# Causal mask of the row maxima in the 16-wide attentions: by TensorE on every own piece instead of by VectorE

## The chip, the cores and the metric

One core of a Trainium2 chip runs the whole program. The metric is the device time of one execution in microseconds; the table below gives the median of three runs. TensorE does the matrix products and writes PSUM, VectorE and ScalarE work on PSUM and SBUF, GpSimd on SBUF, and SyncE issues the copies.

## What is computed

The reference is a chain of sixteen layers on 1024 tokens (batch folded to one in this kernel) of width 256, each with a layer norm ahead and the input added behind. Four of them contain the same kind of attention, with 16 heads of 16 elements: layer 0a, the feed-forward 0 (which runs twice and has an attention inside), and layer 3a. Cut to what matters:

```python
Q, K, V = split_heads(x @ Wq.T), split_heads(x @ Wk.T), split_heads(x @ Wv.T)
scores = jnp.einsum('bhqd,bhkd->bhqk', Q, K) / jnp.sqrt(jnp.float32(HEAD_DIM))
scores = jnp.where(causal, scores, jnp.float32(-jnp.inf))
attn = jax.nn.softmax(scores, axis=-1)
out = jnp.einsum('bhqk,bhkd->bhqd', attn, V)
```

For the softmax the kernel needs the maximum of each row of the masked scores. That maximum is what the change is about.

## The kernel before, in words

narrow_attention() is called once for each of the four attentions, as L0a, L0f (twice) and L3a. It splits queries and keys into three bf16 parts, stacks the parts with copies into qs and ks, and then works in eight units. A unit is a quad of four heads and a half of 512 queries; QUAD_UNITS gives their order. For each unit there are two kinds of work:

- Row maxima. piece() on TensorE makes the scores of 128 queries against up to 512 keys in a bank of a ring of three to four, in bf16 with 96 rows of contraction. find_max() on VectorE reduces the bank to one maximum for each row and frees it. max_pieces() lists the pieces of a unit: for a second half 16 pieces against all the earlier keys, and for every unit 11 own pieces, against the keys of its own half. Own pieces hold a diagonal block and so need the causal mask. The first query tile has one own piece with four heads of 128 keys, the second has two with two heads of 256 keys, the third and fourth have one for each head, with 384 and 512 keys. So there are 8 own pieces of a single head in each unit. part_max() on VectorE then splits a unit's maxima into three bf16 parts, turn_max() (t0 to t7) transposes them on TensorE, keep_max() copies them out and SyncE writes them under qs (place_max()), so that the later scores already have the maximum taken off.
- Scores, exponentials, values. score() on TensorE makes a tile of 128 keys against the queries in one of three banks (s and x in the order), weigh() on ScalarE takes the exponentials, and add_values() on TensorE multiplies them with the values (a in the order), in f32.

The order of all of it is written by narrow_order() as a list of names, which each engine walks through, taking its own part. The pieces m0, m1, ... of a unit stand among the scores of the unit before it; those of units 0 and 1 stand among the projections (p) and values (v) at the start. Around the third own query tile of unit 4 the order reads, with the masked single-head pieces m95 to m102:

```python
m95 s38 m96 x38 m97 s39 x39 m98 s40 m99 x40 m100 s41 m101 x41 a18 a19 m102 s42 x42
```

In unit 5 the same stretch is m122 to m129 and has the four transposes r2 between m124 and m125; unit 3 has r0 in that place. In unit 6 the masked pieces are m133 to m140, of which one stands to about two scores. In unit 7 the order is `m144 a36 a37 m145 m146 s78 m147 s79 m148 s80 m149 x80 m150 s81 x81 a38 a39 m151 s82`. The start reads `p5 m3 m4 m5 p6 m6 m7 m8 v1 m9 m10 p7 m11 v2 m12 m13 t0 m14 m15 m16 v3 m17 m18 m19 m20 s0 x0`; m3 to m10 are the masked single-head pieces of unit 0, m14 to m21 those of unit 1.

Before the change the mask of an own piece is put on in two ways. Pieces with several heads get it on TensorE: behind each head's matmul comes another, ident_bf times causal, added into the last 128 columns (line 1066). Pieces of a single head get it on VectorE: find_max() (line 1358) adds a slice of the tile late to the scores, writes the sums to late_scores and keeps the running maximum. All other pieces are reduced by a plain maximum (line 1362). load_input() makes the constants on GpSimd in the first stage.

Of the kernel before, what the change touches and what calls it, by code (L numbers as in the profile page):

```python
# [6 lines left out]
ALU = mybir.AluOpType  # L7
ACT = mybir.ActivationFunctionType
AX = mybir.AxisListType.X
# [14 lines left out]
class Core:  # L24


    def __init__(self, nc, dram, whole):
        self.nc = nc
        self.dram = dram
        self.old = []  # L30
        self.count = 0
        self.next = self.entered = None
        self.lead = 0
        self.psum = whole.enter_context(nc.psum_tensor("psum", [P, 8, HALF], F32))

        def sb(name, shape, dt=F32):
            return whole.enter_context(nc.sbuf_tensor(name, shape, dt))

        self.x = sb("x", [P, NT, D])
        self.hT = sb("hT", [P, DC, TOK])  # L40
        self.h = sb("h", [P, NT, D])
        self.stats, self.mv = sb("stats", [P, NT, 6]), sb("mv", [P, NT, 2])
        self.scale, self.shift = sb("scale", [P, NT]), sb("shift", [P, NT])
        self.zeros = sb("zeros", [P, HALF], BF16)
        self.powers = sb("powers", [P, 2 * NT])
        self.ident = sb("ident", [P, P])
        self.ident_bf = sb("ident_bf", [P, P], BF16)
        self.causal = sb("causal", [P, P], BF16)
        self.causal_turned = sb("causal_turned", [P, P], BF16)
        self.ones = sb("ones", [P, P])  # L50
        self.late = sb("late", [P, HALF])
        self.ones_rows = nc.dram_tensor("ones_rows", (3, HEADS * TOK), BF16).ap()


# [294 lines left out]
def load_input(core):  # L349

    nc, x = core.nc, core.x
    with Stage(core, "load") as st:
        loaded = [st.sem(f"loaded{q}") for q in range(4)]
        zeroed, ones_set = st.sem("zeroed"), st.sem("ones_set")
        rows_set, rows_stored, powers_set = st.sem("rows_set"), st.sem("rows_stored"), st.sem("powers_set")
        rows = st.sb("rows", [3 * HEADS, TOK], BF16)
        pairs = [st.pair(), st.pair()]
        bank = [core.bank(pairs[q // 2] + q % 2) for q in range(4)]
        following = core.next.open(st, groups=PAIRS, kept_by_dve=(0, 2), last_by_dve=False)
        block = st.opened  # L360

        @block.sync
        def _(sp):
            for q in range(4):
                two = slice(2 * q, 2 * q + 2)
                sp.dma_start(x[:, two, :], core.dram["x"].rearrange("(t p) d -> p t d", p=P)[:, two, :]
                             ).then_inc(loaded[q], 16)
            following.load(sp)
            sp.wait_ge(rows_set, 1)
            sp.dma_start(core.ones_rows.rearrange("i (h t) -> (i h) t", t=TOK), rows[:]).then_inc(rows_stored, 16)  # L370
            sp.wait_ge(rows_stored, 16)
            following.finish(sp)

        @block.vector
        def _(dve):
            nc.vector.memset(core.powers[:, 0:NT], -0.5).then_inc(powers_set, 1)
            nc.vector.memset(core.powers[:, NT:2 * NT], 0.5).then_inc(powers_set, 1)
            nc.vector.memset(rows[:], 1.0).then_inc(rows_set, 1)
            for q in range(4):
                following.find_spread(dve, q, loaded[q])  # L380
            for q in range(4):
                following.keep_dve(dve, q, bank[q])

        @block.scalar
        def _(act):
            for q in range(4):
                act.wait_ge(loaded[q], 16)
                following.row(act, q)
                if q in (1, 3):
                    following.keep_act(act, q, bank[q])  # L390

        @block.tensor
        def _(pe):
            pe.wait_ge(ones_set, 3)
            for q in range(4):
                following.turn(pe, q, bank[q])

        @block.gpsimd
        def _(pool):
            nc.gpsimd.memset(core.ident[:], 0.0).then_inc(zeroed, 1)  # L400
            nc.gpsimd.memset(core.late[:], 0.0).then_inc(zeroed, 1)
            nc.gpsimd.memset(core.ident_bf[:], 0.0).then_inc(zeroed, 1)
            nc.gpsimd.memset(core.causal[:], 0.0).then_inc(zeroed, 1)
            nc.gpsimd.memset(core.causal_turned[:], 0.0).then_inc(zeroed, 1)
            nc.gpsimd.memset(core.ones[:], 1.0).then_inc(ones_set, 1)
            pool.wait_ge(zeroed, 5)
            nc.gpsimd.affine_select(out=core.late[:, HALF - P:], in_=core.late[:, HALF - P:], compare_op=ALU.is_ge,
                                    fill=MASKED, base=0, pattern=[[-1, P]], channel_multiplier=1
                                    ).then_inc(ones_set, 1)
            for t in (core.ident, core.ident_bf):  # L410
                nc.gpsimd.affine_select(out=t[:], in_=t[:], compare_op=ALU.not_equal, fill=1.0, base=0,
                                        pattern=[[-1, P]], channel_multiplier=1).then_inc(ones_set, 1)

            nc.gpsimd.affine_select(out=core.causal[:], in_=core.causal[:], compare_op=ALU.is_ge, fill=MASKED,
                                    base=0, pattern=[[-1, P]], channel_multiplier=1).then_inc(ones_set, 1)
            nc.gpsimd.affine_select(out=core.causal_turned[:], in_=core.causal_turned[:], compare_op=ALU.is_ge,
                                    fill=MASKED, base=0, pattern=[[1, P]], channel_multiplier=-1
                                    ).then_inc(ones_set, 1)
            nc.gpsimd.memset(core.zeros[:], 0.0).then_inc(ones_set, 1)
            pool.wait_ge(powers_set, 2)  # L420
            for q in range(4):
                following.find_scale(pool, q)
            pool.wait_ge(ones_set, 7)


def early(core, stack, name, loads):
# [403 lines left out]
def narrow_attention(core, name, loaded, bias=False, factor=None, first_gated=None):  # L830
# [14 lines left out]
    with Stage(core, name) as st:  # L845
# [21 lines left out]
        whole = [weights[4][:, n, :] for n in range(2)]  # L867
        pool_rest = weights[5][:, 0, :]
        piece_max = [st.sb(f"piece_max{n}", [P, 2, 4, 4]) for n in range(2)]
        late_scores = [st.sb(f"late_scores{n}", [P, HALF]) for n in range(3)]  # L870
        lowest, left = st.sb("lowest", [P, 16]), st.sb("left", [P, 16])
        max_parts = [st.sb(f"max_parts{n}", [P, 3, 16], BF16) for n in range(2)]
        max_rows = [st.sb(f"max_rows{n}", [3 * 16, P], BF16) for n in range(2)]
# [145 lines left out]
        def _(pe):  # L1019
# [31 lines left out]
            def piece(n):  # L1051
                u, i, kh, j0, heads, width = PIECES[n]
                q, half = QUAD_UNITS[u]
                if n == FIRST_PIECE[u]:
                    pe.wait_ge(stacked[q, half], STACKED)
                    if half:
                        pe.wait_ge(stacked[q, 0], STACKED)
                to = own_bank(f"m{n}")
                masks = kh == half and heads > 1
                for e in range(heads):  # L1060
                    h = 4 * q + j0 + e
                    a, b = e * width, (e + 1) * width
                    last = nc.tensor.matmul(to[:, a:b], qs[0:SPLIT, half, h, i * P:(i + 1) * P],  # L1063
                                            ks[0:SPLIT, kh, h, 0:width], start=True, stop=not masks)
                    if masks:
                        last = nc.tensor.matmul(to[:, b - P:b], core.ident_bf[:], core.causal[:],
                                                start=False, stop=True)
                last.then_inc(ring_full, 1)
# [252 lines left out]
        def _(dve):  # L1321
# [28 lines left out]
            def find_max(n):  # L1350
                u, i, kh, j0, heads, width = PIECES[n]
                posted(dve, f"m{n}")
                own = kh == QUAD_UNITS[u][1]
                to, src = piece_max[u % 2][:, int(own), j0:j0 + heads, i], bank_of(f"m{n}")[:, 0:heads * width]
                if own and heads == 1:
                    if n >= 3:
                        taken(dve, f"m{n - 3}")
                    nc.vector.tensor_tensor_reduce(out=late_scores[n % 3][:, 0:width], in0=src,
                                                   in1=core.late[:, HALF - width:], scale=1.0, scalar=-3.0e38,
                                                   op0=ALU.add, op1=ALU.max, accum_out=to).then_inc(ring_free, 1)  # L1360
                else:
                    nc.vector.tensor_reduce(to, src.rearrange("p (e k) -> p e k", e=heads), AX, ALU.max  # L1362
                                            ).then_inc(ring_free, 1)

            def part_max(u):

# [2886 lines left out]
```

## Time and profile before

| | |
|---|---|
| median of 3 runs | 2865.28 us (2863.52 to 2867.5) |
| the profiled execution, its own time | 2867.31 us |
| its span in the profile | 2865.6 us |
| mean granted clock of TensorE | 0.986 of full speed |
| busy: TensorE, VectorE, ScalarE, GpSimd | 95%, 61%, 47%, 24% |
| masked passes on VectorE (line 1358) | 256, and 256 reads of the accumulator |
| mask matmuls on TensorE for the maxima (line 1066) | 256 |

The span is what the profiler saw between the first and the last instruction. A busy TensorE is not one at its peak: the entry of a matmul lasts from its start to its modelled end, and neighbours overlap, so the distance of two starts tells what one costs when they follow closely. "PEld" is the loading of weights, which overlaps the matmuls.

### The profile page before, as it was taken

What the parts mean: (1) busy time and instruction counts of PE and PEld (TensorE: products, weight loads), DVE (VectorE), ACT (ScalarE), POOL (GpSimd) and SP (SyncE); (2) the same over time, 40 slices, a digit from 0 to 9 for tenths busy, and PEclk for the clock granted to TensorE, in tenths of its full rate; (3) what the DMA queues carried; (4) which work ended last, traced back from release to release, by engine and by line L of the source; (5) the groups of instructions that cost most, each with busy time, mean ns of one, the idle gap of its engine ahead of it and who ended that gap; (6) DMA issues with size and microseconds to landing.
All of it is one profiled execution on the core that took longest, in us unless ns stands there. A gap on an engine that the chain in (4) does not pass through costs nothing. (4 is left out here: it accounts for less than half of the span.)

```text
span 2865.6 us, 45708 instructions
## 1 busy us (share of the span) xinstructions
PE 2711.4 (95%) x16625; PEld 1924.5 (67%) x16625; DVE 1735.6 (61%) x3723; ACT 1358.3 (47%) x2811; POOL 677.0 (24%) x815
## 2 busy tenths in 40 slices
PE   7989998989999998999999999899999999989979
PEld 4444465744576886788788888776767677754545
DVE  7758545677446765766666666653333332487487
ACT  3745633536534433433555555543433342336476
POOL 3012002030001532333211110113333330130185
PEclk9999999999999999999999999999999999999999
DMA  3021010020110530432100000000000000120031
GB/s 98 25 58 63 2 52 29 1 65 28 34 33 28 155 111 24 131 111 71 32 23 16 21 16 18 15 26 12 18 12 17 12 36 14 41 69 24 13 101 56
DMA packets 72697, 122.27 MB, mean 43 GB/s; under 512 B 16158, under 2 KB 47232, under 8 KB 72336
## 3 DMA queue, kind: packets, MB, share of 16 engines
q1 hardware_dynamic: 70876, 118.04, 13.7%
q8 instruction: 135, 2.21, 0.3%
q10 hardware_dynamic: 1600, 1.31, 0.3%
q14 instruction: 86, 0.70, 0.1%
HBM read 92.21 MB, written 1.54 MB: 33 GB/s over the span
## 5 line engine op out<-in xcount | busy, mean ns | idle before, releaser
L130 PE MATMUL psum<-L1f_hT_part,L1f_wide 128*128 128x512 f32 x1104 | 269.2, 393 | 10.3 <-DVE L1f_inner L2792 6.1
L236 POOL TENSOR_TENSOR scale<-scale,powers 128x1 f32<-128x1 f32 (+1 forms) x98 | 57.5, 586 | 855.4 <-DVE scale L217 855.4
L1702 ACT ACTIVATE L2b_tanh<-psum,L2b_inverse 128x512 f32<-128x512 f32 x192 | 110.7, 580 | 269.5 <-PE psum L1650 268.1
L130 PEld LDWEIGHTS psum<-L1f_hT_part,L1f_wide 128*128 128x128 f32 x1104 | 201.5, 188 | 54.8 <-DVE L1f_inner L2792 10.7
L2600 POOL TENSOR_TENSOR L1f_inner<-L1f_inner,L1f_weight 128x512 f32<-128x512 f32 x96 | 144.1, 1508 | 263.9 <-DVE L1f_inner L2792 178.0
L1281 ACT ACTIVATE L0f_weights<-psum 128x512 f32<-128x512 f32 (+2 forms) x320 | 157.0, 565 | 95.4 <-PE psum L1097 75.2
L1659 PEld LDWEIGHTS psum<-L2b_v,L2b_weights 128*128 128x128 f32 x1152 | 141.3, 193 | 40.2 <-issue 28.7
L130 PE MATMUL psum<-L1f_down,L1f_inner_part 128*128 128x256 f32 x1152 | 154.3, 285 | 7.8 <-DVE L1f_down L2803 4.2
L130 PEld LDWEIGHTS psum<-L1f_down,L1f_inner_part 128*128 128x128 f32 x1152 | 150.2, 193 | 15.1 <-DVE L1f_inner_part L2808 9.3
L2731 ACT ACTIVATE L1f_gate<-psum 128x512 f32<-128x512 f32 x96 | 57.4, 598 | 211.4 <-PE psum L130 182.5
L2808 DVE TENSOR_TENSOR L1f_inner_part<-L1f_inner,L1f_inner_part 128x512 fp32r<-128x512 f32 x96 | 147.5, 1546 | 9.7 <-ACT L1f_inner_part L2752 9.4
L1650 PE MATMUL psum<-L2b_q,L2b_k 128*128 128x512 f32 (+3 forms) x384 | 149.9, 487 | 1.0 <-DVE L2b_q L1768 0.8
L1659 PE MATMUL psum<-L2b_v,L2b_weights 128*128 128x129 f32 x1152 | 145.2, 278 | 5.8 <-POOL L2b_weights L1568 5.8
L2279 ACT CAST L2a_probsT<-psum 128x512 fp32r<-128x512 f32 (+3 forms) x128 | 65.0, 508 | 147.4 <-PE psum L2131 147.3
L130 PE MATMUL psum<-L2a_k,L2a_q 128*128 128x512 f32 (+3 forms) x576 | 130.7, 356 | 1.7 <-DVE L2a_k L2352 0.9
L2362 DVE TENSOR_REDUCE L2a_negmax<-psum 128x1 f32<-128x512 f32 (+7 forms) x128 | 95.2, 753 | 57.9 <-PE psum L2118 57.8
L1063 PE MATMUL psum<-L0f_ks,L0f_qs 96*128 96x512 bf16 (+3 forms) x384 | 111.5, 332 | 9.9 <-DVE L0f_piece_max L1362 5.6
L2792 DVE TENSOR_TENSOR L1f_inner<-psum,L1f_gate 128x512 f32<-128x512 f32 x96 | 65.9, 689 | 88.8 <-ACT L1f_gate L2731 82.4
L1633 PE MATMUL psum<-hT,L2b_early 128*128 128x512 f32 x248 | 116.5, 593 | 0.9 <-PEq L103 0.9
L1362 DVE TENSOR_REDUCE L0f_piece_max<-psum 128x1 f32<-128x512 f32 (+2 forms) x176 | 108.9, 682 | 12.1 <-PE psum L1063 7.5
L1094 PE MATMUL psum<-L0f_qs,L0f_ks 99*128 99x512 bf16 (+3 forms) x384 | 112.1, 328 | 3.2 <-ACT L0f_weights L1281 2.1
L130 PE MATMUL psum<-L2a_probsT,L2a_v 128*128 128x512 f32 (+3 forms) x576 | 111.6, 348 | 0.7 <-DVE L2a_probsT L2372 0.7
(573 smaller groups left out, 6478.6 us busy)
## 6 DMA issues: line engine op xcount, KB each, us to landing
L1f_w<-in_L1f_w SPq DMA_DIRECT2D x32, 384.0 KB, 3.6
L1f_weight<-combine SPq DMA_DIRECT2D x32, 384.0 KB, 4.4
L1f_weight<-combine SPq DMA_DIRECT2D x32, 256.0 KB, 4.6
scan_spread_b<-bc SPq DMA_DIRECT2D x16, 512.0 KB, 3.7
L0f_qs<-L0f_part SPq DMA_DIRECT2D x96, 64.0 KB, 2.6
experts_early<-in_L1f_w SPq DMA_DIRECT2D x16, 384.0 KB, 4.4
L2b_early<-in_L2b_w SPq DMA_DIRECT2D x16, 384.0 KB, 3.0
L0f_ks<-L0f_part SPq DMA_DIRECT2D x86, 64.0 KB, 2.6
```

What stands on the lines that cost most here:

```text
L130: last = nc.tensor.matmul(to, stationary, moving, start=start and n == 0, stop=stop and n == len(pairs) - 1, skip_group_check=skip)
L1063: last = nc.tensor.matmul(to[:, a:b], qs[0:SPLIT, half, h, i * P:(i + 1) * P], ks[0:SPLIT, kh, h, 0:width], start=True, stop=not masks)
L1094: last = nc.tensor.matmul(to, ks[:, kt // 4, h, kt % 4 * P:(kt % 4 + 1) * P], qs[:, half, h, at:], start=True, stop=not masks)
L1281: nc.scalar.activation(to, src, ACT.Exp, scale=HD ** -0.5).then_inc(exped, 1)
L1362: nc.vector.tensor_reduce(to, src.rearrange("p (e k) -> p e k", e=heads), AX, ALU.max).then_inc(ring_free, 1)
L1633: last = nc.tensor.matmul(to[:], w[e][:, c, at:at + P], hT[:, c, half * HALF:(half + 1) * HALF], start=(c == 0), stop=(c == DC - 1))
L1650: nc.tensor.matmul(ps_scores[u % 3][:, at:], k[e][:, kt * P:(kt + 1) * P], q[e][:, half * HALF + at:(half + 1) * HALF], start=True, stop=T ...
L1659: last = nc.tensor.matmul(ps_out[t % 2][:, 0:P + 1], weights[UNITS.index((kt, t // 4))][:, at:at + P], v[e][:, kt, :], start=(kt == 0), st ...
L1702: nc.scalar.activation(tanhs[u % 3][:, at:], ps_scores[u % 3][:, at:], ACT.Tanh, scale=inverse[e][:, NT + kt:NT + kt + 1]).then_inc(capped, 1)
L2362: nc.vector.tensor_reduce(negmax[:, i:i + 1], ps_scores[i % 2][:, 0:width(i)], AX, ALU.max, negate=True).then_inc(maxed, 1)
L2600: nc.gpsimd.tensor_tensor(inner[u % INNER][:], inner[u % INNER][:], weight[n % SPREAD][:, half * HALF:(half + 1) * HALF], ALU.mult).then_i ...
L2808: nc.vector.tensor_tensor(low[:], inner[u % INNER][:], high[:], ALU.subtract).then_inc(inner_low, 1)
```

## The change

core.late and late_scores go, with their two instructions in the first stage (a memset and a select on GpSimd). piece() puts the mask matmul behind every own piece, those of a single head too; find_max() reduces every piece by the plain maximum. The order of work stays as it is.

```diff
--- before.py
+++ after.py
@@ -48,7 +48,6 @@
         self.causal = sb("causal", [P, P], BF16)
         self.causal_turned = sb("causal_turned", [P, P], BF16)
         self.ones = sb("ones", [P, P])
-        self.late = sb("late", [P, HALF])
         self.ones_rows = nc.dram_tensor("ones_rows", (3, HEADS * TOK), BF16).ap()
 
 
@@ -391,22 +390,18 @@
 
         @block.tensor
         def _(pe):
-            pe.wait_ge(ones_set, 3)
+            pe.wait_ge(ones_set, 2)
             for q in range(4):
                 following.turn(pe, q, bank[q])
 
         @block.gpsimd
         def _(pool):
             nc.gpsimd.memset(core.ident[:], 0.0).then_inc(zeroed, 1)
-            nc.gpsimd.memset(core.late[:], 0.0).then_inc(zeroed, 1)
             nc.gpsimd.memset(core.ident_bf[:], 0.0).then_inc(zeroed, 1)
             nc.gpsimd.memset(core.causal[:], 0.0).then_inc(zeroed, 1)
             nc.gpsimd.memset(core.causal_turned[:], 0.0).then_inc(zeroed, 1)
             nc.gpsimd.memset(core.ones[:], 1.0).then_inc(ones_set, 1)
-            pool.wait_ge(zeroed, 5)
-            nc.gpsimd.affine_select(out=core.late[:, HALF - P:], in_=core.late[:, HALF - P:], compare_op=ALU.is_ge,
-                                    fill=MASKED, base=0, pattern=[[-1, P]], channel_multiplier=1
-                                    ).then_inc(ones_set, 1)
+            pool.wait_ge(zeroed, 4)
             for t in (core.ident, core.ident_bf):
                 nc.gpsimd.affine_select(out=t[:], in_=t[:], compare_op=ALU.not_equal, fill=1.0, base=0,
                                         pattern=[[-1, P]], channel_multiplier=1).then_inc(ones_set, 1)
@@ -420,7 +415,7 @@
             pool.wait_ge(powers_set, 2)
             for q in range(4):
                 following.find_scale(pool, q)
-            pool.wait_ge(ones_set, 7)
+            pool.wait_ge(ones_set, 6)
 
 
 def early(core, stack, name, loads):
@@ -867,7 +862,6 @@
         whole = [weights[4][:, n, :] for n in range(2)]
         pool_rest = weights[5][:, 0, :]
         piece_max = [st.sb(f"piece_max{n}", [P, 2, 4, 4]) for n in range(2)]
-        late_scores = [st.sb(f"late_scores{n}", [P, HALF]) for n in range(3)]
         lowest, left = st.sb("lowest", [P, 16]), st.sb("left", [P, 16])
         max_parts = [st.sb(f"max_parts{n}", [P, 3, 16], BF16) for n in range(2)]
         max_rows = [st.sb(f"max_rows{n}", [3 * 16, P], BF16) for n in range(2)]
@@ -1056,7 +1050,7 @@
                     if half:
                         pe.wait_ge(stacked[q, 0], STACKED)
                 to = own_bank(f"m{n}")
-                masks = kh == half and heads > 1
+                masks = kh == half
                 for e in range(heads):
                     h = 4 * q + j0 + e
                     a, b = e * width, (e + 1) * width
@@ -1352,15 +1346,8 @@
                 posted(dve, f"m{n}")
                 own = kh == QUAD_UNITS[u][1]
                 to, src = piece_max[u % 2][:, int(own), j0:j0 + heads, i], bank_of(f"m{n}")[:, 0:heads * width]
-                if own and heads == 1:
-                    if n >= 3:
-                        taken(dve, f"m{n - 3}")
-                    nc.vector.tensor_tensor_reduce(out=late_scores[n % 3][:, 0:width], in0=src,
-                                                   in1=core.late[:, HALF - width:], scale=1.0, scalar=-3.0e38,
-                                                   op0=ALU.add, op1=ALU.max, accum_out=to).then_inc(ring_free, 1)
-                else:
-                    nc.vector.tensor_reduce(to, src.rearrange("p (e k) -> p e k", e=heads), AX, ALU.max
-                                            ).then_inc(ring_free, 1)
+                nc.vector.tensor_reduce(to, src.rearrange("p (e k) -> p e k", e=heads), AX, ALU.max
+                                        ).then_inc(ring_free, 1)
 
             def part_max(u):
```

## Rows read from the trace of the kernel before

**Rows 1.** The page, part 1: busy time, share of the span, instructions.
```profile
PE 2711.4 (95%) x16625; PEld 1924.5 (67%) x16625; DVE 1735.6 (61%) x3723; ACT 1358.3 (47%) x2811; POOL 677.0 (24%) x815
```

**Rows 2.** Windows of the first two 16-wide attentions; last columns granted clock, DMA share, GB/s.
```profile
28.00:168.00 140.00, 131.83 (x1000) 63.72 (x999) 107.64 (x284) 86.00 (x177) 11.82 (x12) 1.00 0.16 51
203.00:353.00 150.00, 140.43 (x1007) 65.62 (x1008) 111.54 (x290) 86.49 (x179) 24.14 (x24) 0.97 0.15 40
```

**Rows 3.** Waits in 28:168: who for whom, total us, times, longest.
```profile
DVE L0a_late_scores L1358 <- PE psum L1063: 18.7, 18, 2.2
...
PEld psum L1094 <- ACT L0a_weights L1281: 12.7, 32, 1.3
```

**Rows 4.** Groups by line and form in 28:168: busy, mean ns, idle before.
```profile
L1362 DVE TENSOR_REDUCE L0a_piece_max<-psum 128x1 f32<-128x512 f32 x64 | 39.5, 682 | 2.6 <-PE psum L1063 2.6
...
L1358 DVE CUSTOM_DVE_ANT_0 L0a_late_scores<-psum,late 128x512 f32<-128x512 f32 x32 | 20.8, 688 | 8.0 <-PE psum L1063 7.9
...
L1358 DVE DVE_READ_ACCUMULATOR2_ANT L0a_piece_max<- 128x1 f32 x64 | 5.3, 82 | 0.0
```

**Rows 5.** Timeline, VectorE: start, duration, instruction, idle before.
```profile
93.43 6.67 DVE L1362 TENSOR_REDUCE L0a_piece_max<-psum 128x1 f32<-128x512 f32 x11 [0.53 <-PE psum L1063]
...
106.53 0.69 DVE L1358 CUSTOM_DVE_ANT_0 L0a_late_scores<-psum,late 128x512 f32<-128x512 f32 x1
107.14 0.08 DVE L1358 DVE_READ_ACCUMULATOR2_ANT L0a_piece_max<- 128x1 f32 x1
107.14 0.69 DVE L1358 CUSTOM_DVE_ANT_0 L0a_late_scores<-psum,late 128x512 f32<-128x512 f32 x1
```

**Rows 6.** Timeline, TensorE, a piece with four heads of 128 keys.
```profile
99.52 0.22 PE L1063 MATMUL psum<-L0a_ks,L0a_qs 96*128 96x128 bf16 x1
99.58 0.22 PE L1066 MATMUL psum<-causal,ident_bf 128*128 128x128 bf16 x1
99.63 0.22 PE L1063 MATMUL psum<-L0a_ks,L0a_qs 96*128 96x128 bf16 x1
```

**Rows 7.** Timeline, TensorE and ScalarE, unit 4; then unit 5's first masked piece.
```profile
103.48 0.34 PE L1063 MATMUL psum<-L0a_ks,L0a_qs 96*128 96x384 bf16 x1
103.65 0.38 PE L1094 MATMUL psum<-L0a_qs,L0a_ks 99*128 99x512 bf16 x1
...
104.07 4.03 ACT L1281 ACTIVATE L0a_weights<-psum 128x512 f32<-128x512 f32 x8 [1.61 <-PE psum L1094]
...
104.42 0.69 PE L1094 MATMUL psum<-L0a_qs,L0a_ks 99*128 99x512 bf16 x2
...
104.95 0.33 PE L1063 MATMUL psum<-L0a_ks,L0a_qs 96*128 96x384 bf16 x1
...
109.58 2.26 ACT L1281 ACTIVATE L0a_weights<-psum 128x384 f32<-128x384 f32 x5 [1.48 <-PE psum L1097]
...
124.81 0.34 PE L1063 MATMUL psum<-L0a_ks,L0a_qs 96*128 96x384 bf16 x1
```

**Rows 8.** Timeline, unit 6 (TensorE) and unit 7 (ScalarE).
```profile
137.44 0.39 PE L1094 MATMUL psum<-L0a_qs,L0a_ks 99*128 99x512 bf16 x1 [0.22 <-ACT L0a_weights L1281]
...
155.18 2.97 ACT L1281 ACTIVATE L0a_weights<-psum 128x256 f32<-128x256 f32 x6 [1.87 <-PE psum L1097]
```

**Rows 9.** Timeline, TensorE, pieces of units 0 and 1 among the projections.
```profile
34.17 0.76 PE L1063 MATMUL psum<-L0a_ks,L0a_qs 96*128 96x384 bf16 x3
...
42.45 0.34 PE L1063 MATMUL psum<-L0a_ks,L0a_qs 96*128 96x384 bf16 x1 [0.29 <-DVE L0a_piece_max L1362]
```

**Rows 10.** Timeline, TensorE, the first score of unit 2.
```profile
73.47 0.38 PE L1094 MATMUL psum<-L0a_qs,L0a_ks 99*128 99x512 bf16 x1 [0.86 <-DMA L0a_qs<-L0a_max_rows]
```

**Rows 11.** Timeline, GpSimd, its first work after the constants.
```profile
4.99 0.71 POOL L236 TENSOR_TENSOR scale<-scale,powers 128x2 f32<-128x2 f32 x1 [1.11 <-DVE scale L217]
```

**Rows 12.** Timeline, TensorE, the same values in the first and second attention.
```profile
69.24 1.71 PE L1112 MATMUL psum<-L0a_weights,L0a_v 128*32 128x512 f32 x16
...
252.44 3.21 PE L1112 MATMUL psum<-L0f_weights,L0f_v 128*32 128x512 f32 x16
```

## The prediction

> **What bounds the kernel now.** I read the page first. TensorE is busy for 95% of the span, VectorE for 61%, ScalarE for 47% [rows 1]. That is a mean over sixteen layers; the change touches only the four 16-wide attentions, so the next view is their windows, some 150 us each; two of the four are shown [rows 2]. In the first, TensorE is busy 131.8 of 140 us, VectorE 107.6 and ScalarE 86.0. No engine is full, so the chain passes between them, and the timeline has to say who waits at each masked piece.
>
> A masked piece is one head's 128 queries against 384 or 512 keys: PIECES holds eight for each of eight units, so 64 in an attention and 256 in the kernel. Across all of them in the first attention VectorE stood idle 18.7 us in 18 waits for their matmul [rows 3]. At these pieces VectorE mostly waits for TensorE. That is the first sign that moving work from VectorE to TensorE is moving it the wrong way.
>
> **What VectorE is relieved of.** Now a masked maximum is two entries: the pass (688 ns for 512 columns) and a read of the accumulator (82 ns); a plain maximum of 512 is one entry of 682 ns [rows 4]. By duration the change saves 0.688 + 0.082 - 0.682 = 0.09 us a piece, 256 x 0.09 = 23 us of busy time. But durations overlap. Back to back, masked passes of 512 start at 106.53 and 107.14, 0.61 apart; the accumulator read at 107.14 starts together with the next pass [rows 5]. Eleven plain maxima in a row take 6.67 us: (6.67 - 0.68)/10 = 0.60 apart [rows 5]. So where VectorE works without a pause a piece is cheaper by about 0.01 us, and where it works alone the end moves from start + 0.61 + 0.08 = 0.69 to start + 0.68, again 0.01. No row shows a plain maximum of 384, half of the cases; as the fixed part is the same, I take the same 0.01 for it. Bounds: 0.01 and 0.09 us a piece. I take 0.01, since the starts show it directly.
>
> **What TensorE gets.** Each masked piece gains a 128-column matmul of ident_bf and causal with its weight load. The same pair stands already behind the narrow pieces: at 99.52 a piece of 128, at 99.58 its mask, at 99.63 the next piece [rows 6]. That is 0.057 us a step; the entry's 0.22 is latency, and the weight load lies under the matmul before it. No row shows a mask behind a piece of 384 or 512; the bounds are this 0.057 and twice as much, 0.114, the price at half the clock (rows 12 show the clock's effect); I take the step, the nearest row. Total: 64 x 0.057 = 3.65 us an attention, 256 x 0.057 = 14.6 us. The Trainium skill, "TensorE: Matmul & The Clock Gate", section "Back-to-back issue gap", puts a sustained stream of load and matmul pairs of 128 columns at about 81 ns each; by that the total would be 20.7 us. The rows disagree with 0.057, and the measurement decides.
>
> **How much of the 3.65 us is on the path**, unit by unit in the first attention.
>
> *Unit 4* (pieces m95 to m102), step by step [rows 7]. m95 at 103.48 stands ahead of the first score at 103.65, and ScalarE's burst of eight exponentials starts at 104.07 after 1.61 us of idling for that score: 0.057 passes through. The next two pieces come ahead of the second score of the row at 104.42; it starts at 104.42 + 0.69 - 0.38 = 104.73, held by ScalarE, where the array was free at 104.42 + 0.22 = 104.64. With this 0.09 of slack the shift there is 3 x 0.057 - 0.09 = 0.08. m98 (104.95) is again followed by a score held by ScalarE: back to ScalarE's own 0.057. From then on a 384-column step of 0.17 (103.48 to 103.65) makes 0.22 for 512 columns, and a period is piece 0.22, score 0.22, mask 0.057 = 0.50, against ScalarE's (4.03 - 0.6)/7 = 0.49: no slack. m99, m100 and m101 each add 0.057, making 0.23 as TensorE reaches the values. The values need exponentials long finished, so they start 0.23 late; m102 follows, and the score behind it ends ScalarE's idle 1.48 us at 109.58: 0.285 late. Less 0.01 for VectorE: 0.28 of 0.46 us.
>
> *Units 3 and 5* are alike but have four transposes (r0 in unit 3, r2 between m124 and m125 in unit 5), which take away ScalarE's lead; four pieces in place of three then add in full: 0.36 each. *Unit 7*: m145 and m146 stand ahead of the score that ScalarE has idled 1.87 us for at 155.18 [rows 8], and from there to the values the order holds one piece to each score, so that every mask adds: 0.45. *Unit 6* has few pieces for each score; TensorE waits for ScalarE behind them (0.22 at 137.44, rows 8), and only those just behind the values count: 0.20. *Unit 0* lies between projections, with VectorE waiting for its pieces; its three pieces at 34.17 take 0.76 us, where two steps of 0.16 and an end of 0.33 would be 0.65, so some 0.13 is slack: 0.46 - 0.13 = 0.33 [rows 9]. *Unit 1*: m14 to m16 wait for VectorE to free a bank (0.29 us at 42.45, rows 9), after which m16 and m17 count: 0.10. *Unit 2*: behind it a score stands at 73.47 and waits 0.86 us for the copy of a unit's maxima, which SyncE issues after the stacking copies in its queue [rows 10]; what TensorE loses before is taken up there: 0.
>
> Sum: 0.33 + 0.10 + 0 + 0.36 + 0.28 + 0.36 + 0.20 + 0.45 = 2.08 us, 57% of 3.65. The four attentions share one order, so 4 x 2.08 = 8.3 us; less 0.3 us for VectorE's hundredths where it is the pace (units 1 and 2, and the end of each unit): **+8.0 us**.
>
> **The other edits cost nothing.** In the first stage GpSimd loses a memset and a select. It is done with its setup early and at 4.99 has idled 1.11 us for VectorE's first spread [rows 11]; if that cover were gone, the gain would be the two instructions, under 1.11 us. The buffers late_scores and their wait on the piece three before hold nothing up: that wait is on VectorE's own, older work. No DMA and no place in a queue changes.
>
> **Against which time.** The profiled execution took 2867.31 us (span 2865.6 and 1.7 around it); the median of the three timed runs is 2865.28. 2867.3 + 8.0 = 2875.3 for a profiled run, 2865.3 + 8.0 = **2873.3** as median.
>
> **Rivals.** A change under 0.2%, 5.7 us, can hardly be told from none.
>
> *A, more is hidden, no change.* If the shifts before the first score are taken up elsewhere (each unit ends in a chain of small VectorE steps and a turn), only the contiguous stretches count: units 3, 5 and 7, 0.9 us an attention. Time +3.6: 2868.9. For it: PE's weight loads show 12.7 us of waits for ScalarE in this attention [rows 3]. Against it: those waits start from an event that is itself late. Chance 0.24.
>
> *B, the mask is dearer.* If the slack I subtract is not there, the full 14.6 us falls on the path: 2879.9. A step of 0.114 at the exposure of 57% gives 16.6 - 0.3 = 16.3, 2881.6. Against it: rows 6. Chance 0.10. The Trainium skill's 81 ns (page and section as above) lies in this direction; by it and the 57% the change would be +11.8 - 0.3 = +11.5, 2876.8, inside the range.
>
> *C, faster: VectorE is the pace.* If the accumulator read holds VectorE's release back by its full length, each piece on VectorE's path saves 0.09 us and hides its mask. With a share s of pieces on that path the change is 8.3(1 - s) - 23s. It becomes faster by more than 5.7 us from s = 0.45; at 0.6 it is -10.5, 2854.8. For it: units 1 and 2 (s = 0.25, though unit 2 sits behind SyncE's queue). Against it: 18.7 us of VectorE waiting, and the starts 0.61 apart. Chance 0.06.
>
> *The clock.* Granted is 1.00 over the first attention and 0.97 over the second [rows 2]. There, behind waits of TensorE for VectorE, the values that take 1.71 us at 2.4 GHz in the first took 3.21 [rows 12], nearly twice, as at 1.2 GHz: 1.5 us lost. More matmuls in it could keep the clock at 2.4 GHz, other timing could move one in; I count plus or minus 3 us and no mean.
>
> **Chances and range.** The forecast holds 0.60, with 2870 to 2877 of its own. Range: down to 2864 (A with the clock's help), up to 2882 (B); what is left out is nearly all of C, 0.06, and some 0.05 above. Slower by over 0.2%, above 2871.0: nine tenths of the forecast and all of B, with a little of A, 0.66. Within: 0.27. Faster: C and a hundredth, 0.07.
>
> **What the profile after would show.** L1066 goes from 256 entries to 512 at 219 ns; the accumulator reads are gone; VectorE's busy time falls by some 23 us with next to nothing in the span. The first masked piece of unit 5 stands 21.33 us behind that of unit 4 (124.81 and 103.48, rows 7); I expect 21.6 (0.28 more). ScalarE's idle before its bursts grows by the hundredths above. The wait at 73.47 shrinks by about as much as TensorE arrives later. Masks more than 60 ns apart show B; unit 4 unchanged shows A; shorter unit 0 to 2 shows C. The prediction is wrong if a piece's shift does not survive the wait for ScalarE behind it, or if VectorE's starts come closer than 0.60.

## The result, and the profile after

The changed kernel takes 2874.99 us (median of 9 runs, 2870.15 to 2879.75) against 2864.73 us of the kernel before (9 runs). The ratio is 1.0036, with a 95% interval of 1.0026 to 1.0046: slower by 10.3 us, between 7.4 and 13.2. The forecast was +8.0, 2873.3.

The page after, part 1. Beside [rows 1]: 256 matmuls more on TensorE, 256 instructions fewer on VectorE. VectorE's busy time is down by 7 us and not by the 23 foretold; one plain maximum takes as long as one masked pass did (682 ns for 688), and the accumulator reads that went had overlapped neighbouring passes, so that they added little to the busy time.

```profile
PE 2720.8 (95%) x16881; PEld 1941.8 (68%) x16881; DVE 1728.5 (60%) x3467; ACT 1360.5 (47%) x2811; POOL 675.3 (23%) x813
```

The windows of the first two attentions, to be read beside [rows 2] (each 2 to 4 us wider, as the stages are longer; the columns are those of rows 2). The granted clock of the second is 0.99 where it was 0.97, which comes back below.

```profile
28.00:170.00 142.00, 134.61 (x1061) 67.26 (x1060) 106.08 (x219) 86.22 (x176) 11.86 (x12) 1.00 0.15 49
203.00:357.00 154.00, 143.81 (x1084) 70.52 (x1083) 111.15 (x228) 88.20 (x181) 24.14 (x24) 0.99 0.17 42
```

The waits of the first attention after, for [rows 3]. VectorE now waits 24.0 us for a mask matmul. That line holds the narrow pieces too; for the single-head pieces alone it is 9.6 + 11.5 = 21.1 us (the groups below) where it waited 18.7 us for the piece: VectorE had time, and has more of it. TensorE's weight loads wait less for ScalarE, 8.7 us for 12.7: the slack in front of the scores is what the masks used up.

```profile
DVE L0a_piece_max L1349 <- PE psum L1060: 24.0, 20, 2.2
...
PEld psum L1088 <- ACT L0a_weights L1275: 8.7, 24, 0.8
```

Groups by form there, for [rows 4]. A plain maximum of 384, of which no row of before told, takes 550 ns against 553 for its masked twin (line 1358, 128x384, in the same view of before).

```profile
L1349 DVE TENSOR_REDUCE L0a_piece_max<-psum 128x1 f32<-128x512 f32 x96 | 60.1, 682 | 12.6 <-PE psum L1060 9.6 <-PE psum L1057 2.8
L1060 PE MATMUL psum<-causal,ident_bf 128*128 128x128 bf16 x128 | 24.7, 219 | 0.0
...
L1349 DVE TENSOR_REDUCE L0a_piece_max<-psum 128x1 f32<-128x384 f32 x32 | 16.3, 550 | 11.6 <-PE psum L1060 11.5
```

Unit 4 in the timeline of the changed kernel, TensorE, for [rows 7].

```profile
104.68 0.34 PE L1057 MATMUL psum<-L0a_ks,L0a_qs 96*128 96x384 bf16 x1
104.85 0.22 PE L1060 MATMUL psum<-causal,ident_bf 128*128 128x128 bf16 x1
104.91 0.38 PE L1088 MATMUL psum<-L0a_qs,L0a_ks 99*128 99x512 bf16 x1
105.13 0.33 PE L1057 MATMUL psum<-L0a_ks,L0a_qs 96*128 96x384 bf16 x1
...
106.97 0.22 PE L1060 MATMUL psum<-causal,ident_bf 128*128 128x128 bf16 x1
107.03 0.38 PE L1088 MATMUL psum<-L0a_qs,L0a_ks 99*128 99x512 bf16 x1
...
108.51 1.92 PE L1106 MATMUL psum<-L0a_weights,L0a_v 128*32 128x512 f32 x16
...
126.29 0.34 PE L1057 MATMUL psum<-L0a_ks,L0a_qs 96*128 96x384 bf16 x1
```

The mask stands between piece and score and takes 0.06 (104.85 to 104.91; 106.97 to 107.03 behind a piece of 512). From the first masked piece to the values it is 108.51 - 104.68 = 3.83 us. The first masked piece of unit 5 follows after 126.29 - 104.68 = 21.61 us, where 21.33 stood and 21.6 was foretold.

ScalarE in the same stretch. Its burst of eight exponentials is as long as before (4.03), it starts later after a longer wait, 1.66 for 1.61, and the wait behind the burst grew from 1.48 to 1.72: TensorE comes later to the first score behind the values.

```profile
105.33 4.03 ACT L1275 ACTIVATE L0a_weights<-psum 128x512 f32<-128x512 f32 x8 [1.66 <-PE psum L1088]
111.07 1.25 ACT L1275 ACTIVATE L0a_weights<-psum 128x384 f32<-128x384 f32 x3 [1.72 <-PE psum L1091]
```

**A clock for each unit.** VectorE copies out the maxima of each unit once, eight times an attention. These starts cut an attention into units. First the kernel before, then the changed one, first attention, timeline of VectorE.

```profile
42.91 0.20 DVE L1387 COPY L0a_max_rows<-psum 48x128 bf16<-48x128 bf16 x1
53.63 0.21 DVE L1387 COPY L0a_max_rows<-psum 48x128 bf16<-48x128 bf16 x1
69.98 0.20 DVE L1387 COPY L0a_max_rows<-psum 48x128 bf16<-48x128 bf16 x1
92.09 0.21 DVE L1387 COPY L0a_max_rows<-psum 48x128 bf16<-48x128 bf16 x1
113.42 0.21 DVE L1387 COPY L0a_max_rows<-psum 48x128 bf16<-48x128 bf16 x1
133.90 0.20 DVE L1387 COPY L0a_max_rows<-psum 48x128 bf16<-48x128 bf16 x1
152.44 0.20 DVE L1387 COPY L0a_max_rows<-psum 48x128 bf16<-48x128 bf16 x1
160.74 0.20 DVE L1387 COPY L0a_max_rows<-psum 48x128 bf16<-48x128 bf16 x1
```

```profile
43.20 0.20 DVE L1374 COPY L0a_max_rows<-psum 48x128 bf16<-48x128 bf16 x1
54.09 0.21 DVE L1374 COPY L0a_max_rows<-psum 48x128 bf16<-48x128 bf16 x1
70.50 0.20 DVE L1374 COPY L0a_max_rows<-psum 48x128 bf16<-48x128 bf16 x1
93.30 0.20 DVE L1374 COPY L0a_max_rows<-psum 48x128 bf16<-48x128 bf16 x1
114.90 0.20 DVE L1374 COPY L0a_max_rows<-psum 48x128 bf16<-48x128 bf16 x1
135.74 0.20 DVE L1374 COPY L0a_max_rows<-psum 48x128 bf16<-48x128 bf16 x1
154.45 0.20 DVE L1374 COPY L0a_max_rows<-psum 48x128 bf16<-48x128 bf16 x1
163.21 0.20 DVE L1374 COPY L0a_max_rows<-psum 48x128 bf16<-48x128 bf16 x1
```

The delay grows line by line: 0.29, 0.46, 0.52, 1.21, 1.48, 1.84, 2.01, 2.47. What each unit adds is the difference of neighbours. Each kernel was profiled twice (experiment 4). In the first attention the intervals between copies repeat from profile to profile of one kernel to within some 0.02 us, except that of unit 3 (22.11 and 21.94 before, 22.80 and 22.83 after). Unit 4's is 21.33 or 21.34 in all four attentions of both profiles of before, 21.60 to 21.62 in both of the changed one. They are the yardstick of the experiments below.

Unit 0 has no interval, and its figure is less sure: the first copy stands at 42.91 and 42.04 in the two profiles of before, at 43.20 and 43.30 in the two after. Counted from the first piece of the attention on TensorE, the first copy comes 13.87 and 13.61 us later before, 14.25 both times after, so that unit 0 adds 0.38 or 0.64 by this count, of which eight masks of 0.057 can be 0.46 at most.

| unit | 0 | 1 | 2 | 3 | 4 | 5 | 6 | 7 | sum |
|---|---|---|---|---|---|---|---|---|---|
| foretold | 0.33 | 0.10 | 0 | 0.36 | 0.28 | 0.36 | 0.20 | 0.45 | 2.08 |
| first attention, measured | 0.29 | 0.17 | 0.06 | 0.69 | 0.27 | 0.36 | 0.17 | 0.46 | 2.47 |

### The profile page after: what moved, and what is told of

Its sections match the earlier page's. It is cut to its first block and busy times, and to the rows that moved or that the text cites. A ratio compares the mean times of both kernels' runs of the same rounds, so it can differ in the third digit from the quotient of the medians.

```text
span 2874.6 us, 45705 instructions
## 1 busy us (share of the span) xinstructions
PE 2720.8 (95%) x16881; PEld 1941.8 (68%) x16881; DVE 1728.5 (60%) x3467; ACT 1360.5 (47%) x2811; POOL 675.3 (23%) x813
## 5 line engine op out<-in xcount | busy, mean ns | idle before, releaser
L1349 DVE TENSOR_REDUCE L0f_piece_max<-psum 128x1 f32<-128x512 f32 (+3 forms) x304 | 182.0, 655 | 56.2 <-PE psum L1060 50.6
```

## The experiments

Each was timed in alternation with the kernel before on the same chip; differences are of those medians.

**1. TensorE's half alone.**

```diff
-                masks = kh == half and heads > 1
+                masks = kh == half
```

The rest is the kernel before; the mask is then added twice.

> The kernel before with the 256 mask matmuls of the single-head pieces added on TensorE, while VectorE keeps its masked pass and the accumulator read (the mask is then added twice). It is the TensorE half of the change alone. My theory (TensorE's 57 ns are the whole cost, VectorE's part is worth 0.01 us a piece): 8.3 us slower than before in all, against 10.3 us measured for the change, and in the profile of the first attention a loss of about 2.5 us from its first unit to its last, as in the changed kernel. Rival, VectorE's relief is worth something that hid part of the cost: clearly slower than the changed kernel, by up to 23 us if each accumulator read counted. Rival, the cost lies in a longer wait of VectorE for the mask: the same as the changed kernel.

Measured: 2873.79 against 2865.40, +8.4 us; ratio 1.0032 (1.0020 to 1.0044). Unit 4's interval is 21.62, unit 5's 20.83 and unit 7's 8.76, as in the changed kernel. The TensorE half is the change. That the relief of VectorE hid part of the cost is ruled out for units 4 to 7 to two hundredths. In units 1 and 2 the relief shows: their intervals are 10.96 and 16.46 here, 10.89 and 16.41 in the changed kernel.

**2. VectorE's half alone.** The changed kernel, the mask left out on the single-head pieces, so that the maxima are taken over more keys:

```diff
-                masks = kh == half
+                masks = kh == half and heads > 1
```

> The changed kernel without the mask on the single-head pieces: a plain maximum over all keys of the piece, nothing added on TensorE (the row maxima are then taken over more keys than the causal ones). It is the VectorE half of the change alone. My theory: 0.3 us faster than before, which is no difference. Rival, VectorE is the pace at many pieces: 5 us or more faster (0.09 us for each of 256 pieces is 23 us at most). Rival, dropping the buffers and the constants in the first stage shifts something by itself: slower than before though nothing was added.

Measured: 2864.34 against 2865.40; ratio 0.9997 (0.9988 to 1.0006), no difference. In the first attention units 1 and 2, where VectorE is the pace, are each 0.06 us shorter (10.66 for 10.72, 16.29 for 16.35): eight pieces at 0.008 us. Units 4 to 7 are shorter by 0.02 at most. So 0.01 us a piece holds and 0.09 does not, and dropping the buffers and constants costs nothing that can be told from none.

**3. The mask twice**, in the changed kernel, on single-head pieces:

```diff
+                        if heads == 1:
+                            nc.tensor.matmul(to[:, b - P:b], core.ident_bf[:], core.causal[:],
+                                             start=False, stop=False)
```

> The changed kernel with the mask matmul of the single-head pieces issued twice, so 512 added matmuls in place of 256. My theory: slack in front of TensorE is used up by the first mask, so the second is exposed at more than 57 percent: 8.3 to 14.6 us slower than the changed kernel, in the first attention 2.5 to 3.65 us more. Rival, the change's cost is not the matmuls' time but something that comes once (a wait, a phase of the clock): less than 4 us more.

Measured: 2880.86, +15.5 us against before; ratio 1.0054 (1.0040 to 1.0067); the changed kernel on the same chip took 2875.64, so the second mask adds 5.2 us, below what I expected. By units the expectation holds: unit 4 grows by 0.43 more (22.03 for 21.60), unit 5 by 0.43, unit 7 by 0.44 of a full 0.46, that is, the slack is used up. Of unit 3 the second and third attentions tell, 22.07 and 22.06 for 21.62 or 21.63 in the changed kernel's third: 0.43. With 0.38 for unit 0 (first copy at 43.58 for 43.20), 0.17, 0.11 and 0.18 in units 1, 2 and 6, the second mask is worth 2.57 of its full 3.65 us, the lower end of what I expected. In the first attention, from first to last copy, it comes to 1.0 us only, because unit 3's interval shrank there from 22.80 to 22.06; this is SyncE's queue, below. The total of 5.2 carries the uncertainty of two medians, some 4 us, so that the total alone does not refute the rival of under 4 us; the units do.

**4. The changed kernel again, and the kernel before again** (no edit).

> The changed kernel once more, for a second profile. The profile already seen loses 3.4 us in the four attentions and 5.6 us in layers that the change does not touch, and its stretches at half clock lie elsewhere than in the kernel before. If those places come from the timing of the start alone, they lie elsewhere again in this profile, the first attention (no half clock in it) again ends 2.5 us later than before, and the total is again about 10 us above before. If they belong to the change, they lie where they lay: none behind unit 2 of the second to fourth attention, and some 2 us lost between the first and second feed-forward 0.

> The kernel before once more, for a second profile of it. The time is that of before. In question is the clock: the first profile has a half-clock stretch behind unit 2 in each of the second to fourth attentions, and the interval from the maxima of unit 2 to those of unit 3 is 22.75 to 22.89 us there; with the masks it is 21.6 to 21.7 in some of them. If the masks keep the clock up there, this profile has the stretch again in at least two of the three. If it is the phase of the run, it has it in one or none.

Measured: after again 2875.64 against 2865.40, ratio 1.0036 (1.0022 to 1.0050); before again 2863.45 against 2864.06, ratio 0.9999. The profiled execution of the changed kernel had a span of 2864.5 this time, 10 us under the first, at a mean clock of 0.991 for 0.987. The four attentions, from their first copy of maxima to their last ScalarE copy, are 545.1 and 544.4 us in the two; all the rest is 2329.5 and 2320.1. In the first profile of before they are 542.0 and 2323.6. So a single profile can't be charged for what lies outside: the 5.9 us that the first profile lost in unchanged layers are not shown to be the change's. The profile of before again has the stretch behind unit 2 in the second and third attentions (22.90 and 22.84), not in the fourth (21.52): by what I had written, the masks keep the clock up. The next experiment speaks against it.

**5. By unit.** The new mask only in some units:

```diff
-                masks = kh == half and heads > 1
+                masks = kh == half and (heads > 1 or u in (3, 5, 7))
...
-                if own and heads == 1:
+                if own and heads == 1 and u not in (3, 5, 7):
```

> The kernel before with the new mask (TensorE adds it, plain maximum) only in units 3, 5 and 7, 96 of the 256 pieces. My theory by the prediction's units: 4 x (0.36 + 0.36 + 0.45) = 4.7 us slower than before; in the first attention the distances between the copies of the maxima grow only over those units, by about 0.7 (as in the changed kernel's profile), 0.35 and 0.46 us. Rival, the loss is spread by masks and not by place: 96/256 of 10.2 = 3.8 us. Rival, a shift of one unit is taken up in the next: under 2 us.

> The kernel before with the new mask only in units 0, 1, 2, 4 and 6, 160 of the 256 pieces. My theory: 4 x (0.33 + 0.10 + 0 + 0.28 + 0.20) = 3.6 us slower, less than with the 96 pieces of units 3, 5 and 7. Rival, spread by masks: 160/256 of 10.2 = 6.4 us. The two kernels together should give the change's 10.2 us if the units add up.

Measured: units 3, 5 and 7: 2867.98 against 2864.06, +3.9; ratio 1.0012 (1.0002 to 1.0022). Units 0, 1, 2, 4 and 6: 2869.82, +5.8; ratio 1.0019 (1.0010 to 1.0029). Together 9.7, near the change's 10.3. The totals are too uncertain to tell place from number of masks; the eleven runs with units 3, 5 and 7 lie in two groups, six from 2865.6 to 2868.0 and five from 2872.2 to 2876.0, so that their median is less sure than it looks. The intervals tell: with units 3, 5 and 7 the first attention has 10.72, 16.34, 22.15, 21.33, 20.83, 18.56, 8.76, so units 5 and 7 grow by 0.35 and 0.46 and unit 4 not at all; with the others 10.90, 16.40, 22.16, 21.61, 20.46, 18.70, 8.30, the reverse. Nothing spreads to a neighbour.

This pair also bears on the clock. With units 3, 5 and 7, no mask is added in the same attention ahead of the stretch behind unit 2, and yet it is gone in the second and third attention. Windows of before, at the values of [rows 12], then of this kernel; the third column from the end is the granted clock:

```profile
252.00:256.00 4.00, 4.00 (x23) 0.89 (x21) 1.98 (x5) 0.60 (x1) 0.00 (x0) 0.57 0.26 86
```

```profile
252.00:256.00 4.00, 4.00 (x33) 1.62 (x32) 3.47 (x8) 1.48 (x4) 0.00 (x0) 1.00 0.27 85
...
2580.00:2584.00 4.00, 4.00 (x25) 1.39 (x24) 1.90 (x3) 2.81 (x6) 0.00 (x0) 0.61 0.31 108
```

The same instructions run at 1.00 in the second attention, and the fourth has a stretch at 0.61 instead. The stretch lies just behind a place where TensorE waits for VectorE (0.94 us at 250.90 in before, 0.93 us at 250.54 here), and whether the clock falls there differs by kernel and, in the fourth attention, by run. In the fourth, before has 22.75 us with it and 21.52 without: 1.2 us. In the second and third, 22.84 to 22.90 stand against 21.26 with units 0, 1, 2, 4 and 6 (second attention, no new mask in unit 3 either): 1.6 us. So added masks ahead of it in the attention are not needed for it to stay away.

Yet it comes and goes by a pattern. In the second and third attentions all three profiles without a new mask have it (both of before and experiment 2's: 22.84 to 22.90), and none of the six with new masks (both of the changed kernel, experiments 1 and 3, and this experiment's two). What decides it is not shown. It matters for the sum: the changed kernel wins some 1.6 us back in each of these two attentions.

**6. The opposite of the change.** The narrow pieces' masks go to VectorE too, a masked pass for each head (in some variants only in some units):

```diff
-                masks = kh == half and heads > 1
+                masks = False
...
-                if own and heads == 1:
+                if own:
...
+                    for e in range(heads):
+                        a, b = e * width, (e + 1) * width
+                        last = nc.vector.tensor_tensor_reduce(out=late_scores[n % 3][:, a:b], in0=src[:, a:b],
+                            in1=core.late[:, HALF - width:], scale=1.0, scalar=-3.0e38, op0=ALU.add, op1=ALU.max,
+                            accum_out=piece_max[u % 2][:, 1 if own else 0, j0 + e, i:i + 1])
+                    last.then_inc(ring_free, 1)
```

> The opposite of the change: the kernel before with the 256 mask matmuls of the narrow own pieces (four heads of 128 keys, two of 256) taken off TensorE too; VectorE does a masked pass for each head in place of one plain maximum for the bank. It still computes the same. TensorE loses 64 x 0.057 = 3.65 us an attention; VectorE gains per unit about 2 x 0.08 + 0.2 = 0.36 us, 2.9 us an attention. My theory (TensorE paces, VectorE waits): faster than before by 3 to 8 us. Rival, VectorE becomes the pace in units 1 and 2 and wherever a bank is awaited: no change or slower, with the loss in the intervals of units 1 to 3.

> As all_vector, but units 1 and 2 keep their narrow masks on TensorE. It takes away the one place where VectorE was the pace: the interval of unit 2 should be 16.35 us again (16.77 in all_vector, and 18.23 and 18.06 with a half-clock stretch in it in the second and third attention). Expected 1.6 us (4 x 0.42) to 4.5 us faster than all_vector. Rival, the half-clock stretches move elsewhere and nothing is gained: the time of all_vector.

> As all_vector, but only in units 3, 4, 5 and 7; in units 0, 1, 2 and 6 the narrow pieces keep their masks on TensorE as in the kernel before. In the profile of all_vector the first attention won 0.48 us in the interval that holds unit 4's pieces, 0.13 in unit 5's and 0.66 in unit 7's, and lost 0.42 in unit 2's and 0.18 in unit 6's. My theory: the wins stay and the losses go, so about 4 x (0.5 + 0.48 + 0.13 + 0.66) = 7 us faster than before and about 3 us faster than all_vector. Rival, what a unit wins is taken up by the next unit's wait: the intervals win as said but the time is that of all_vector (2.9 us under before) or of before.

| masks of the narrow pieces by VectorE in | median, before | ratio (95%) |
|---|---|---|
| all units | 2861.73, 2864.06 | 0.9990 (0.9980 to 1.0000) |
| all but 1 and 2 | 2860.95, 2863.75 | 0.9990 (0.9981 to 0.9999) |
| 3, 4, 5, 7 | 2859.91, 2863.75 | 0.9987 (0.9978 to 0.9996) |

The last beats both kernels: 3.8 us under before and 15 us under the changed one. I expected 7. Its first attention, timeline of VectorE, last six copies:

```profile
69.67 0.21 DVE L1391 COPY L0a_max_rows<-psum 48x128 bf16<-48x128 bf16 x1
91.18 0.21 DVE L1391 COPY L0a_max_rows<-psum 48x128 bf16<-48x128 bf16 x1
112.02 0.21 DVE L1391 COPY L0a_max_rows<-psum 48x128 bf16<-48x128 bf16 x1
132.01 0.21 DVE L1391 COPY L0a_max_rows<-psum 48x128 bf16<-48x128 bf16 x1
150.74 0.21 DVE L1391 COPY L0a_max_rows<-psum 48x128 bf16<-48x128 bf16 x1
158.37 0.21 DVE L1391 COPY L0a_max_rows<-psum 48x128 bf16<-48x128 bf16 x1
```

Unit 4 takes 20.84 for 21.33, unit 5 19.99 for 20.48, unit 7 7.63 for 8.30. Unit 6 keeps its loss of 0.19 (18.73 for 18.54) although its masks are back on TensorE, so that loss is not from its own masks. What came back with them is unit 5's interval, which was 20.35 with the masks of all units on VectorE: the narrow pieces of unit 6 stand ahead of unit 5's copy. With all units on VectorE unit 2 took 16.77 for 16.35, as VectorE is the pace there; with units 1 and 2 spared it is 16.34. The half-clock stretch that the kernel with all units on VectorE had there in the second and third attention (18.23 and 18.06) went with it, but the time moved by less than can be told. From its first copy to its last ScalarE copy, the first attention is 131.0 us for 133.0. Over all four it is 532.2 us for 542.0 and 539.3 in the two profiles of before. The timed 3.8 has an interval of 1.1 to 6.3. Where the rest is, is open.

## Why the prediction was right

**The side and the size.** Slower, 10.3 measured for 8.0 foretold, and the mechanism as told: masks of 0.057 us on a TensorE that paces. Experiment 1 alone gives 8.4, experiment 2 no difference. That the total came as near as this is in part luck, as said under what stays open.

**The price of a mask** was taken from the step behind narrow pieces. It holds behind 384 and 512 columns (0.06), and the bound of 0.114 did not come up at full clock. The Trainium skill's 81 ns from "TensorE: Matmul & The Clock Gate", section "Back-to-back issue gap", is not what this stream shows: 0.06 us stands from the mask's start to the next in the rows above, 0.057 in [rows 6].

**VectorE's part** was taken from the starts, 0.01 us a piece, and is 0.008. The step that failed here is a by-product: "VectorE's busy time falls by some 23 us". It fell by 7.1. The page's busy time counts overlapping entries once, so the sum of durations was the wrong sum even for that; it did not enter the forecast.

**The exposure, unit by unit, in the first attention** was right to 0.01 us in units 4, 5 and 7 and to 0.07 in units 1, 2 and 6; unit 0's 0.33 stands against 0.29, 0.38 or 0.64, by the count and the profile taken (its slack, 0.76 - 0.65, is 0.11 and not the 0.13 subtracted). The step from one attention to four was taken without looking at the others, and unit 1 is not alike there: in the second and third its interval is 14.48 to 14.63 in before and 14.57 to 14.62 after, so that its masks add next to nothing. Unit 3 was foretold at 0.36 and its interval grew by 0.69. The masks' part is 0.37: the first score of unit 2 starts 0.84 us later than before (74.31 for 73.47), the maxima of unit 3 1.21 later, and 1.21 - 0.84 = 0.37. With units 3, 5 and 7 alone that score stands at 73.07 and the maxima at 92.06, so 92.06 - 73.07 = 18.99, where before has 92.09 - 73.47 = 18.62, again 0.37.

**The remaining part of unit 3's interval is SyncE's queue, and what I said of it failed.** I wrote that what TensorE loses before 73.47 is taken up there and that its wait shrinks. It grew, for [rows 10]:

```profile
74.31 0.38 PE L1088 MATMUL psum<-L0a_qs,L0a_ks 99*128 99x512 bf16 x1 [1.17 <-DMA L0a_qs<-L0a_max_rows]
```

The queue's own rows tell why, changed kernel, timeline of SyncE's queue:

```profile
54.32 0.76 SPq L958 DMA_DIRECT2D L0a_qs<-L0a_max_rows  x1
55.12 3.75 SPq L944 DMA_DIRECT2D L0a_qs<-L0a_part  x6
58.92 5.08 SPq L944 DMA_DIRECT2D L0a_ks<-L0a_part  x6
64.05 3.78 SPq L944 DMA_DIRECT2D L0a_qs<-L0a_part  x6
67.87 4.13 SPq L944 DMA_DIRECT2D L0a_ks<-L0a_part  x6
72.04 0.74 SPq L958 DMA_DIRECT2D L0a_qs<-L0a_max_rows  x1
```

The 24 stacking copies between two sets of maxima keep the queue at work from 54.32 to 72.04. They can only start once unit 1's maxima are sent, in the same queue, so the 0.46 us that units 0 and 1 lose pass through it in full. Here it is a link of the chain, no cushion. On top, six copies take 3.75 to 5.08 us to issue, and the run from one set to the next is 17.72 us here, 17.34 in before (53.86 to 71.20), 16.99 with units 3, 5 and 7 (53.80 to 70.79) and 16.51 with the mask twice (54.88 to 71.39), where the score, at 73.66, no longer waits for it. It does not follow the number of masks. Here it gave 0.38 us more. Of this, 0.06 only covers what unit 2 had lost, which the wait did take up as foretold, and 0.32 is left in the interval: 0.37 + 0.32 = 0.69. Since I counted units 0 and 1 in full and unit 2 at nothing, the sum was not hurt.

**The rivals.** A (more is hidden) is refuted by units 3 to 7, whose shifts survive each wait for ScalarE behind them. B (the full 14.6) is refuted for the first mask; the second comes near it in units 3, 4, 5 and 7 (0.43 or 0.44 of 0.46), not in the others. C (VectorE paces) is right about places, units 1 and 2, and wrong about the price, 0.008 for 0.09. The clock was booked as plus or minus 3 us and no mean; the profiles give it a side, some 3 us in favour of the changed kernel in the second and third attentions.

**What stays open.** The forecast took four times the first attention. All four can be read in the profiles, from an attention's first piece on TensorE to its last ScalarE copy:

| attention | before | before again | experiment 2 | changed | changed again | experiment 1 |
|---|---|---|---|---|---|---|
| first | 146.9 | 146.5 | 146.6 | 149.5 | 149.5 | 149.5 |
| second | 153.3 | 153.1 | 153.2 | 153.5 | 154.0 | 153.1 |
| third | 150.3 | 150.3 | 150.2 | 151.1 | 151.0 | 151.1 |
| fourth | 152.0 | 147.5 | 147.5 | 151.7 | 150.7 | 150.3 |
| sum | 602.5 | 597.4 | 597.4 | 605.7 | 605.2 | 604.0 |

The first three columns have no new mask, the last three have them all. In the first attention 2.9 us are lost, in the second and third only 0.3 and 0.8, since there the stretch at half clock is gone. On average the four lose 5.9 us. The unit account gives 4 x 2.15 = 8.6 us (0.29 + 0.17 + 0.06 + 0.37 + 0.27 + 0.36 + 0.17 + 0.46 = 2.15); less the 3 us of clock this is about what the attentions show, and the forecast of 8.0 left that clock out. That its total still came near the timed one is in part luck. The timed 10.3 has 7.4 at the lower end of its interval, so by this some microseconds, at least 1.5, lie elsewhere, if the profiled executions are like the timed ones. The rest of the execution takes 2263.1 to 2267.2 us in the first three profiles and 2259.3 to 2269.2 in the last three, which scatters too much to show them. A candidate is a stretch at a granted clock of 0.79 at 476 to 484 us in an unchanged layer of the changed kernel's first profile, absent from its second and from before; how often it occurs wasn't measured. Where those us are, and whether the change causes them, is open.

## What to carry to other kernels

Before a reduction is relieved of work at the cost of a matmul, look at who waits at that very instruction: here VectorE idled 18.7 us at the masked maxima, so its relief was worth next to nothing, and of the added 57 ns each on TensorE about six tenths lasted to the end of the first attention. Price back-to-back instructions by the distance of their starts and not by their durations; an accumulator read of 82 ns cost 8. And when single intervals repeat to 0.02 us while the total scatters by 5, put markers into the timeline and compare these, unit by unit; but read every repetition of a stage before multiplying one by four, since here two of four attentions had a stretch at half clock to lose.

## What was not expected of the hardware

The scatter of the whole, some 10 us between two profiled executions of one kernel (2874.6 and 2864.5), lies almost all outside the four attentions (2329.5 and 2320.1), while intervals at full clock inside agree to 0.02 us. The stretch at half clock behind unit 2 follows a wait of TensorE and comes and goes with the kernel and the run, without any change to the work in it, at 1.2 to 1.6 us each. SyncE's issue of six equal copies took between 3.75 and 5.13 us, which made the run of 24 copies in the first attention 16.51 to 17.72 us long from kernel to kernel; between before and the changed kernel it moved a score by 0.38 us. And the pair of masked pass and accumulator read costs VectorE as much as a plain maximum of the same bank, to within 0.01 us.
